# A two-layer decoder on one core: in-place activations, joined products, and other places in the step lists

## The chip, the core and the metric

The kernel runs on one core of a Trainium2 chip, as a single program. The metric is the device time of that program in microseconds. The engines are TensorE (PE; its weight loads are listed apart as PEld), VectorE (DVE), ScalarE (ACT), GpSimd (POOL) and SyncE (SP, which here only issues DMAs). The median of three runs before the change is 2692.59 us (2692.17 to 2693.38).

## The reference

Tokens `x` are 2 batches of 1024, 256 wide, float32. There are two layers of three blocks, each added to a residual stream, each on a LayerNorm of it:

```python
x = x + L0_attn(layernorm(x), ...)             # A: gated delta rule, 4 heads, short convolution of 4 taps
x = x + L0_xattn(layernorm(x), ctx_1024, ...)  # B: cross attention, 16 heads of 64, 154 context tokens
x = x + L0_ffn(layernorm(x), ...)              # C: 8 experts, each takes its own best 512 tokens, GELU, 256-1024-256
x = x + L1_attn(layernorm(x), ...)             # D: rotary attention in a window of 128, 16 heads
x = x + L1_xattn(layernorm(x), ctx_1024, ctx_1024, mask, ...)  # E: masked cross attention, 16 heads of 16
x = x + L1_ffn(layernorm(x), ...)              # F: best 8 of 32 experts per token and 2 shared ones, SiLU, 128 wide
```

In A, `short_conv(hidden @ W)` gives queries, keys and values: a product, then four taps along time, then SiLU. In C, `I` are an expert's best 512 tokens by gate score, and `hid = gelu(ex @ W1 + b1)`.

## The kernel before

The residual stream stays in SBUF as `X`, 16 tiles of 128 tokens. The kernel is six stages, A to F, one after the other. Each has a list `order` of named steps, written out by hand; every engine walks that list in its order and does its share of each step, so an engine that waits in one step delays all its later ones. Semaphores join the engines; a PSUM bank is an object with one semaphore `filled` and one `emptied`.

**LayerNorm** is four steps for a pair of tiles: `stat` (DVE, L257 and L260), then `ln_pool` on POOL (L279, L224 and a Newton step, L213 to L216) for the reciprocal root in `rs`, `norm` (DVE, `xn`, L270), and `ln` (PE, four transposes, L291, then an ACT copy to `XT`, L299). The first LayerNorm waits on POOL for all constants (`const_in`, 48), since the exponent -0.5 is one of them. A LayerNorm for the next stage is spread through the list of the stage before.

**Stage A** (to 810 us) makes 16 channels by 8 blocks of convolution products. One is line 576: for each batch and each half of the 256 inputs a matmul of 128 columns, 4 in all, which the trace records as 8 (each float32 matmul is two records). ACT and DVE then do the taps (L924, L925, L777). Between these run the triangular solves on 64x64 blocks (L664, L674, L678). In the first block four products stand between LayerNorm steps.

**Stage B** (810 to 1170) begins with 8 `value` products (L1232), each beside a LayerNorm, and the first queries (L1241); then scores (L1257) and so on in units.

**Stage C** (1170 to 1488): gate logits, a search of ten digits for each expert's threshold (L1686 on DVE, L1612 on PE), then per expert a `pick` (L1724 makes one-hot tiles, L1629 multiplies them with token numbers), a gather of the tokens by indirect DMA (POOL, L1833), and `turn` (transposes L1636, ACT copy, and a subtraction, L1744, for the low half). Products are taken in three parts with operands split into a high and a low half (`fp32r`); `split` makes the halves of weights on POOL (L1822) or DVE (L1738). An expert's 8 parts, f = 0 to 7, are each `up` (L1569), GELU and `down`, two parts later:

```python
c.e.activation(hid[j % NH_][:, :], b.ap, ACT.Gelu, bias=b1[:, j:j + 1])
c.e.activation(hp[j % NH_][:, 0], b.ap, ACT.Gelu, bias=b1[:, j:j + 1]).then_inc(b.emptied, 1)
```

The first is the whole result in SBUF, the second its high half; DVE (L1752) subtracts the two for the low half.

**Stages D and E** (1488 to 1808 to 2077) are attention in steps of a group g: scores, a maximum on DVE (D: L2040, E: L2373 and L2376), exponentials on ACT, transposes (E: L2315) with DVE copies (E: L2382), products with the values (E: L2326). Each step list also carries `norm` and `ln` for the stage that follows.

**Stage F** (2077 to 2694) runs all 34 experts over all tokens: 136 parts of `up` and `down`, all on line 2559. Weights are split by ACT (L2709) and POOL (L2738), tokens by ACT and DVE. The choice of 8 of 32 is made on DVE in 8 pieces, `route`, one per part from the fourth part on; it is needed from part 8, since the shared experts come first. DVE adds results to `X` (L2694, L2696).

## Time and profile before

| | us |
|---|---|
| median of the runs (n = 3) | 2692.59 |
| profiled execution, its own time | 2696.3 |
| its span | 2694.5 |
| PE busy | 2315.0 (86%) |
| DVE busy | 1662.2 (62%) |
| ACT busy | 1166.5 (43%) |
| POOL busy | 740.6 (27%) |

The granted TensorE clock was 0.929 of full speed on average. The page's row of that clock by 40 slices reads `8699999999999999967999799998997899999999`: it is under full speed in the first slices and around the stage borders. Busy shares are an average over stages with different limits; the chain of waits, which is followed back from the last instruction, tells which engine was last in each stretch. A span is some 2 us shorter than the execution's own time; both are of one execution.

### The profile page before, as it was taken

What the parts mean: (1) busy time and instruction counts of PE and PEld (TensorE: products, weight loads), DVE (VectorE), ACT (ScalarE), POOL (GpSimd) and SP (SyncE); (2) the same over time, 40 slices, a digit from 0 to 9 for tenths busy, and PEclk for the clock granted to TensorE, in tenths of its full rate; (3) what the DMA queues carried; (4) which work ended last, traced back from release to release, by engine and by line L of the source; (5) the groups of instructions that cost most, each with busy time, mean ns of one, the idle gap of its engine ahead of it and who ended that gap; (6) DMA issues with size and microseconds to landing.
All of it is one profiled execution on the core that took longest, in us unless ns stands there. A gap on an engine that the chain in (4) does not pass through costs nothing.

```text
span 2694.5 us, 63114 instructions
## 1 busy us (share of the span) xinstructions
PE 2315.0 (86%) x26243; PEld 1928.3 (72%) x26243; DVE 1662.2 (62%) x3601; ACT 1166.5 (43%) x3232; POOL 740.6 (27%) x875
## 2 busy tenths in 40 slices
PE   4689989998988999946888588888876899999998
PEld 3678878887865777735887366666655688888887
DVE  4566666667644555556774455556665777777776
ACT  2544444444323545412554356556665333333332
POOL 2334243423323333332665433420001011111110
PEclk8699999999999999967999799998997899999999
DMA  2201010101003000021342300000000000000000
GB/s 87 66 10 34 26 34 10 34 26 38 34 2 105 9 17 17 17 71 41 101 106 32 99 2 1 2 2 1 2 1 8 18 18 24 25 26 27 26 7 32
DMA packets 87821, 83.41 MB, mean 31 GB/s; under 512 B 27248, under 2 KB 83312, under 8 KB 86128
## 3 DMA queue, kind: packets, MB, share of 16 engines
q1 hardware_dynamic: 81392, 70.98, 8.5%
q0 software_dynamic: 6144, 8.39, 1.8%
q8 instruction: 208, 3.41, 0.5%
q14 instruction: 77, 0.63, 0.1%
HBM read 68.71 MB, written 10.65 MB: 29 GB/s over the span
## 4 chain that ended last, share of the span: by engine, by line
PE 66%; DVE 17%; POOL 6%; issue 5%; ACT 4%; DMA 1%; DVEq 0%; SPq 0%; ACTq 0%; POOLq 0%
PE bank L2559 20%; PE bank L1569 5%; PE bank L576 4%; PE bank L664 3%; PE bank L678 2%; PE bank L674 2%; PE bank L1291 2%; PE bank L1268 2%; PE bank L1241 2%; DVE d_mx L2040 2%; PE bank L1281 2%; DVE e_P L2373 1%; DVE a_acc L777 1%; PE bank L2315 1%; PE bank L2326 1%
## 5 line engine op out<-in xcount | busy, mean ns | idle before, releaser
L2559 PE MATMUL bank<-f_XH,f_wp 128*128 128x512 f32 x1088 | 366.6, 398 | 8.0 <-POOL f_wp L2738 8.0
L777 DVE SCALAR_TENSOR_TENSOR a_acc<-a_praw,a_convw,a_acc 128x256 f32<-128x256 f32 x345 | 205.0, 595 | 101.3 <-ACT a_acc L925 93.0
L2559 PEld LDWEIGHTS bank<-f_XH,f_wp 128*128 128x128 f32 x1088 | 209.3, 192 | 51.1 <-POOL f_wp L2738 8.6
L2559 PEld LDWEIGHTS bank<-f_wp,f_Hp 128*128 128x128 f32 x1632 | 214.6, 192 | 23.8 <-DVE X L2696 9.6
L2559 PE MATMUL bank<-f_wp,f_Hp 128*128 128x256 f32 x1632 | 219.1, 284 | 12.2 <-DVE X L2696 8.9
L2559 PE MATMUL bank<-f_XL,f_wp 128*128 128x512 f32 x544 | 216.7, 398 | 0.0
L2694 DVE SCALAR_TENSOR_TENSOR X<-bank,f_w,X 128x256 f32<-128x256 f32 x512 | 211.3, 475 | 0.0
L2738 POOL TENSOR_TENSOR f_wp<-wa,f_wp 128x768 fp32r<-128x768 f32 x34 | 62.7, 1845 | 511.4 <-ACT f_wp L2709 511.4
L2732 ACT ACTIVATE f_Hp<-f_H 128x512 fp32r<-128x512 f32 x136 | 85.9, 632 | 222.9 <-DVE f_H L2681 222.9
L576 PE MATMUL bank<-XT,wa 128*128 128x128 f32 x1024 | 165.2, 313 | 7.5 <-ACT a_acc L925 6.6
L2730 ACT ACTIVATE f_G<-bank 128x512 f32<-128x512 f32 x136 | 81.4, 599 | 166.8 <-PE bank L2559 166.8
L576 PEld LDWEIGHTS bank<-XT,wa 128*128 128x128 f32 x1024 | 142.3, 216 | 15.8 <-ACT a_acc L925 7.6
L2683 DVE TENSOR_TENSOR f_Hp<-f_H,f_Hp 128x512 fp32r<-128x512 f32 x136 | 94.1, 692 | 94.9 <-ACT f_Hp L2732 94.9
L664 PE MATMUL bank<-wa 64*64 64x64 f32 x2560 | 108.1, 229 | 44.4 <-DVE wa L866 31.2
L2040 DVE TENSOR_REDUCE d_mx<-bank 128x2 f32<-128x512 f32 (+1 forms) x128 | 75.2, 650 | 115.1 <-PE bank L1976 115.1
L2681 DVE TENSOR_TENSOR f_H<-bank,f_G 128x512 f32<-128x512 f32 x136 | 94.0, 691 | 82.4 <-PE bank L2559 79.0
L291 PE MATMUL bank<-wide,xn 128*128 128x128 f32 x192 | 39.3, 341 | 114.3 <-DVE xn L270 114.3
L664 PEld LDWEIGHTS bank<-wa 64*64 64x64 f32 x2560 | 89.2, 139 | 63.1 <-DVE wa L866 38.1
L2110 ACT ACTIVATE d_P<-bank,d_mx 128x256 f32<-128x256 f32 (+1 forms) x256 | 95.1, 479 | 74.5 <-DVE d_mx L2040 74.5
L992 ACT ACTIVATE wa<-bank 128x256 f32<-128x256 f32 x160 | 58.6, 386 | 157.0 <-PE bank L664 156.2
L279 POOL TENSOR_SCALAR rs<-mv 128x2 f32<-128x2 f32 x48 | 10.9, 226 | 415.9 <-DVE mv L260 403.9
L1390 POOL TENSOR_TENSOR b_P<-b_P,b_rec 128x616 f32<-128x616 f32 x64 | 77.6, 1212 | 172.4 <-DVE b_rec L1328 172.4
(370 smaller groups left out, 5657.2 us busy)
## 6 DMA issues: line engine op xcount, KB each, us to landing
wa<-in_c_w SPq DMA_DIRECT2D x64, 256.0 KB, 3.2
wa<-in_f_gu SPq DMA_DIRECT2D x34, 256.0 KB, 2.8
wb<-grown SPq DMA_DIRECT2D x4, 1536.0 KB, 6.9
a_KQg<-grown SPq DMA_DIRECT2D x4, 1536.0 KB, 6.3
wa<-in_f_d SPq DMA_DIRECT2D x34, 128.0 KB, 2.9
a_E<-decays SPq DMA_DIRECT2D x16, 256.0 KB, 4.8
X<-in_x SPq DMA_DIRECT2D x4, 512.0 KB, 5.7
wa<-in_a_wqkv SPq DMA_DIRECT2D x1, 2048.0 KB, 12.1
```

The costliest lines, as they stand in the source:

```text
L576: i = t.e.matmul(b.ap[:, bb * BT_:(bb + 1) * BT_], wqkv[:, j, c * P:(c + 1) * P], XT[:, j, bb * T + n * BT_:bb * T + (n + 1) * BT_], start ...
L664: i = t.e.matmul(heads(b.ap)[both(bb), h, :], nt[c % 2][both(bb), h, :], xx[c % 2][both(bb), 0, h, :], start=True, stop=True, tile_positio ...
L777: i = v.e.scalar_tensor_tensor(A_, praw[:, c, :, j:j + BT_], convw[:, c, j:j + 1], A_, ALU.mult, ALU.add)
L1569: i = t.e.matmul(out_, lhsT[x], rhs[y], start=first and n == 0, stop=last and n == 2, skip_group_check=True)
L2040: v.e.tensor_reduce(mx[:, of(g, r), :], pair(b.ap)[:, :, lo:], AX, ALU.max, negate=True).then_inc(max_ready.sem, 1)
L2110: i = c.e.activation(Pm[of(g, r)][:, j, lo:], pair(b.ap)[:, j, lo:], ACT.Exp, bias=mx[:, of(g, r), j:j + 1])
L2559: i = t.e.matmul(out_, lhsT[x], rhs[y], start=n == 0 and k == 0, stop=n == 2 and k == nk - 1, skip_group_check=True)
L2681: v.e.tensor_tensor(hid[i][:, :], up.ap, gate[i][:, :], ALU.mult).then_inc(up.emptied, 1)
L2683: v.e.tensor_tensor(hp[i][:, 1], hid[i][:, :], whole(hp[i][:, 0]), ALU.subtract).then_inc(parts_ready.sem, 1)
L2694: i = v.e.scalar_tensor_tensor(X[:, n, :], part, w_[:, n, e_:e_ + 1], X[:, n, :], ALU.mult, ALU.add)
L2730: c.e.activation(gate[i][:, :], b.ap, ACT.Silu).then_inc(b.emptied, 1)
L2732: c.e.activation(hp[i][:, 0], hid[i][:, :], ACT.Copy).then_inc(high_ready.sem, 1)
```

## The change

It has nine edits, by stage. Line numbers in the changed kernel are 5 to 12 higher than before.

- A, start: -0.5 is a tile that POOL sets; the identity has its own DMA; the LayerNorm steps stand together, and the four products after `z` and `gates` 0.
- A: one convolution matmul covers both batches (2 matmuls of 256 columns for 4 of 128). Two late `gate` steps stand one place earlier.
- B: all `stat` steps first, then per pair `value`, `ln`, `norm` and a query.
- C, start: four weight splits ahead of the logits. The pick goes tile by tile with a wait per quarter; token numbers come already multiplied by 128.
- C: GELU's high half first, then GELU in place in the PSUM bank; DVE subtracts from the bank, and the buffer `hid` is gone. `turn` at f = 4 and 5 instead of 5 and 6.
- D, start: the wait for the window mask is at the first score; DVE's cast and POOL's memsets stand behind the first LayerNorms.
- D and E: each `ln` for the stage that follows stands one step later than its `norm`.
- E to F: the last `stat` is in F behind the first split; the last `norm` and `ln` one part later; `route` from part 4, two pieces per part.

```diff
+        minus_half = sb("minus_half", [P, 1])
...
-            for i in (0, 2, 1, 3):
+            def load_x(i):
                 tiles = slice(i * NT // 4, (i + 1) * NT // 4)
                 y.e.dma_start(X[:, tiles, :], a["x"].rearrange("b (t p) d -> p (b t) d", p=P)[:, tiles, :]).then_inc(x_in[i], 16)
-            y.e.dma_start(wide[:, :], a["wide"]).then_inc(const_in, 16)
+
+            load_x(0)
+            y.e.dma_start(wide[:, 0:P], a["wide"][:, 0:P]).then_inc(ident_in, 16)
+            for i in (2, 1, 3):
+                load_x(i)
+            y.e.dma_start(wide[:, P:], a["wide"][:, P:]).then_inc(const_in, 16)
...
-            half = const("half")
+            half = minus_half[:, :]
...
-            g.wait_ge(const_in, 48)
+            g.wait_ge(half_ready, 1)
...
-            t.wait_ge(const_in, 48)
+            t.wait_ge(ident_in, 16)
...
-                order += [(what, "A", halves[i - 2]) for what in ("norm", "ln")] * (i > 1) + conv0[i - 6:i - 5] * (i > 5)
-            order += [("z",), ("gates", 0)] + [("gates", 1)] + conv0[4:7] + [("gates", 2), ("rows",)] + conv0[7:11] + silu0[0:4]
+                order += [(what, "A", halves[i - 2]) for what in ("norm", "ln")] * (i > 1)
+            order += [("z",), ("gates", 0)] + conv0[0:4] + [("gates", 1)] + conv0[4:7] + [("gates", 2), ("rows",)] + conv0[7:11] + silu0[0:4]
...
+                    first -= what == "gate" and t > NC - 3
...
-                        for bb in range(B):
-                            for j in range(KD):
-                                i = t.e.matmul(b.ap[:, bb * BT_:(bb + 1) * BT_], wqkv[:, j, c * P:(c + 1) * P],
-                                               XT[:, j, bb * T + n * BT_:bb * T + (n + 1) * BT_],
-                                               start=j == 0, stop=j == KD - 1, skip_group_check=True)
+                        for j in range(KD):
+                            xt = XT[:, j, :].rearrange("p (b t) -> p b t", b=B)[:, :, n * BT_:(n + 1) * BT_]
+                            i = t.e.matmul(b.ap[:, 0:B * BT_].rearrange("p (b t) -> p b t", b=B), wqkv[:, j, c * P:(c + 1) * P], xt,
+                                           start=j == 0, stop=j == KD - 1, skip_group_check=True)
...
-            lns = [[("stat", "B", i)] * (i < NT // 2) + [("norm", "B", i - 2), ("ln", "B", i - 2)] * (i > 1) for i in range(NT // 2 + 2)]
-            for i in range(NT // 2):
-                order += lns[i] + [("value", i // 4, i // 2 % 2, i % 2)]
-                if i > 2:
-                    order += [("query", 0, m) for m in range(MT) if i > 6 or m == i - 3]
-            order = [s for i, s in enumerate(order) if s not in order[:i]]
-            order += lns[-2] + lns[-1]
+            order += [("stat", "B", i) for i in range(NT // 2)] + [("norm", "B", 0), ("ln", "B", 0), ("norm", "B", 1)]
+            for i in range(MT):
+                order += [("value", i // 4, i // 2 % 2, i % 2)] + [("ln", "B", i + 1)] * (i + 1 < NT // 2)
+                order += [("norm", "B", i + 2)] * (i + 2 < NT // 2) + [("query", 0, i)]
...
-                    if f in (5, 6) and more:
-                        work += [("turn", e_ + 1, 2 * (f - 5))]
+                    if f in (4, 5) and more:
+                        work += [("turn", e_ + 1, 2 * (f - 4))]
...
-            order = [("norm", "C", NT // 2 - 1), ("ln", "C", NT // 2 - 1), ("logits",), ("flip",), ("split", 0), ("split", 1), ("split", 2), ("split", 3)]
+            order = [("norm", "C", NT // 2 - 1), ("ln", "C", NT // 2 - 1), ("split", 0), ("split", 1), ("split", 2), ("split", 3), ("logits",), ("flip",)]
...
+                        for n in range(NT):
+                            t.wait_ge(coded.sem, coded.at[e_, 4 * n // NT])
+                            for m in range(SB):
...
-                        v.step(v.e.scalar_tensor_tensor(idf[:, e_, :], picked[:, :, 0], float(P), idf[:, e_, :], ALU.mult,
-                                                        ALU.add)); v.settle()
-                        v.e.tensor_copy(idx[:, e_, :], idf[:, e_, :]).then_inc(index_ready.sem, 1)
+                        v.e.tensor_tensor(idx[:, e_, :], picked[:, :, 0], idf[:, e_, :], ALU.add).then_inc(index_ready.sem, 1)
...
-                        emptied(v, *s)
-                        v.e.tensor_tensor(hp[j % NH_][:, 1], hid[j % NH_][:, :], whole(hp[j % NH_][:, 0]),
-                                          ALU.subtract).then_inc(parts_ready.sem, 1)
+                        v.wait_ge(hidden.sem, hidden.at[e_, f])
+                        v.e.tensor_tensor(hp[j % NH_][:, 1], b.ap, whole(hp[j % NH_][:, 0]), ALU.subtract).then_inc(b.emptied, 1)
...
-                        c.e.activation(hid[j % NH_][:, :], b.ap, ACT.Gelu, bias=b1[:, j:j + 1])
-                        c.e.activation(hp[j % NH_][:, 0], b.ap, ACT.Gelu, bias=b1[:, j:j + 1]).then_inc(b.emptied, 1)
+                        c.e.activation(hp[j % NH_][:, 0], b.ap, ACT.Gelu, bias=b1[:, j:j + 1])
+                        c.e.activation(b.ap, b.ap, ACT.Gelu, bias=b1[:, j:j + 1]).then_inc(hidden.sem, 1)
...
-                    order += [("norm", "E", (g - 7) // 4), ("ln", "E", (g - 7) // 4)]
+                    order += [("norm", "E", (g - 7) // 4)]
+                if g % 4 == 0 and 0 <= g // 4 - 2 < NT // 2 - 1:
+                    order += [("ln", "E", g // 4 - 2)]
...
+                        t.wait_ge(window_ready, 1)
...
+                    if s == ("keys", 0, 0):
+                        v.e.tensor_copy(smallb[:, :], small[:, 0:3 * P]).then_inc(window_ready, 1)
...
+                    if s == ("project", 0):
+                        for i in range(2):
...
-                    order += [("norm", "F", (g - 7) // 4), ("ln", "F", (g - 7) // 4)]
+                    order += [("norm", "F", (g - 7) // 4)]
+                if g % 4 == 0 and 0 <= g // 4 - 2 < NT // 2 - 1:
+                    order += [("ln", "F", g // 4 - 2)]
...
-            order = [("split", 0)] + [("high", q) for q in range(3)]
+            order = [("split", 0), ("high", 0), ("stat", "F", NT // 2 - 1), ("high", 1), ("high", 2)]
             for p in range(NP + LAG):
-                if p == 1:
+                if p == 2:
                     order += [("norm", "F", NT // 2 - 1), ("ln", "F", NT // 2 - 1)]
-                elif p == 2:
+                elif p == 3:
                     order += [("high", 3), ("logits",)]
-                elif p == 3:
+                elif p == 4:
                     order += [("flip",)]
                 if p < NP:
                     if p % 4 == 2 and p // 4 + 1 < NEX:
                         order += [("split", p // 4 + 1)]
                     order += [("up", p)]
-                    if 3 <= p < 3 + ROUTE:
-                        order += [("route", p - 3)]
+                    if 4 <= p < 4 + ROUTE // 2:
+                        order += [("route", 2 * (p - 4)), ("route", 2 * (p - 4) + 1)]
...
-                for j in range(NEX):
+                for s in order:
+                    if s[0] == "stat":
+                        ln_pool(g, s)
+                    if s[0] != "split":
+                        continue
+                    j = s[1]
```

PE at the start of stage B before. L1232 is `value`, L291 the LayerNorm transposes, L1241 the queries:

```order
L1221 MATMUL bank<-ctxT,wa 128x308 x16
L1232 MATMUL bank<-wa,ctxT 77x512 x4
L291 MATMUL bank<-wide,xn 128x128 x4
L1232 MATMUL bank<-wa,ctxT 77x512 x2
L291 MATMUL bank<-wide,xn 128x128 x4
L1232 MATMUL bank<-wa,ctxT 77x512 x2
L1241 MATMUL bank<-XT,wb 128x256 x2
L291 MATMUL bank<-wide,xn 128x128 x4
L1232 MATMUL bank<-wa,ctxT 77x512 x2
L1241 MATMUL bank<-XT,wb 128x256 x2
```

And the same place after, where the lines are L1237, L296 and L1246:

```order
L1226 MATMUL bank<-ctxT,wa 128x308 x16
L296 MATMUL bank<-wide,xn 128x128 x4
L1237 MATMUL bank<-wa,ctxT 77x512 x2
L296 MATMUL bank<-wide,xn 128x128 x4
L1246 MATMUL bank<-XT,wb 128x256 x2
L1237 MATMUL bank<-wa,ctxT 77x512 x2
L296 MATMUL bank<-wide,xn 128x128 x4
L1246 MATMUL bank<-XT,wb 128x256 x2
L1237 MATMUL bank<-wa,ctxT 77x512 x2
```

The transposes that stood alone between two values now have a query behind them, and the first LayerNorm stands ahead of the values.

DVE in stage C over one expert, before; L1752 is the subtraction for GELU's low half, L1744 the turn:

```order
L1752 TENSOR_TENSOR c_hp<-c_h,c_hp 128x512
L1724 TENSOR_SCALAR c_oh<-c_iota,c_rk 128x512 x4
L1738 TENSOR_TENSOR c_wp<-wa,c_wp 128x1024
L1752 TENSOR_TENSOR c_hp<-c_h,c_hp 128x512
L1724 TENSOR_SCALAR c_oh<-c_iota,c_rk 128x512 x4
L1744 TENSOR_TENSOR c_exT<-bank,c_exT 128x2x256
L1752 TENSOR_TENSOR c_hp<-c_h,c_hp 128x512
L1744 TENSOR_TENSOR c_exT<-bank,c_exT 128x2x256
L1752 TENSOR_TENSOR c_hp<-c_h,c_hp 128x512 x2
```

And after, where they are L1755 and L1747:

```order
L1755 TENSOR_TENSOR c_hp<-bank,c_hp 128x512
L1729 TENSOR_SCALAR c_oh<-c_iota,c_rk 128x512 x4
L1741 TENSOR_TENSOR c_wp<-wa,c_wp 128x1024
L1747 TENSOR_TENSOR c_exT<-bank,c_exT 128x2x256
L1755 TENSOR_TENSOR c_hp<-bank,c_hp 128x512
L1729 TENSOR_SCALAR c_oh<-c_iota,c_rk 128x512 x4
L1747 TENSOR_TENSOR c_exT<-bank,c_exT 128x2x256
L1755 TENSOR_TENSOR c_hp<-bank,c_hp 128x512 x3
```

The subtraction reads `bank` where it read `c_h`, and the turn stands ahead of the subtraction and the one-hot tiles that it followed.

PE in stage E before; L291 is the LayerNorm of stage F, L2315 the turn of the exponentials, L2345 the output product:

```order
L2315 MATMUL bank<-wide,e_P 77x128 x8
L2334 MATMUL bank<-wide,e_OT 128x128 x2
L291 MATMUL bank<-wide,xn 128x128 x4
L2315 MATMUL bank<-wide,e_P 77x128 x8
L2326 MATMUL bank<-e_PT,e_V 32x128 x16
L2304 MATMUL bank<-e_KT,e_Q 128x154 x8
L2340 MATMUL bank<-wide,e_AO 128x128 x2
L2315 MATMUL bank<-wide,e_P 77x128 x8
L2334 MATMUL bank<-wide,e_OT 128x128 x2
L2345 MATMUL bank<-wb_d,e_AOT 128x256 x2
```

And after, L296, L2322 and L2352:

```order
L2322 MATMUL bank<-wide,e_P 77x128 x8
L2341 MATMUL bank<-wide,e_OT 128x128 x2
L2322 MATMUL bank<-wide,e_P 77x128 x8
L2333 MATMUL bank<-e_PT,e_V 32x128 x16
L2311 MATMUL bank<-e_KT,e_Q 128x154 x8
L2347 MATMUL bank<-wide,e_AO 128x128 x2
L2322 MATMUL bank<-wide,e_P 77x128 x8
L2341 MATMUL bank<-wide,e_OT 128x128 x2
L2352 MATMUL bank<-wb_d,e_AOT 128x256 x2
L296 MATMUL bank<-wide,xn 128x128 x4
L2322 MATMUL bank<-wide,e_P 77x128 x8
```

The LayerNorm stands behind the output product of the next step.

## Rows read from the trace of the kernel before

**Rows 1.** The page: the chain of waits by engine.

```profile
PE 66%; DVE 17%; POOL 6%; issue 5%; ACT 4%; DMA 1%; DVEq 0%; SPq 0%; ACTq 0%; POOLq 0%
```

**Rows 2.** By stretch: us, busy us of PE, PEld, DVE, ACT, POOL, PEclk, DMA.

```profile
110.00:810.00 700.00, 630.44 (x12623) 559.78 (x12623) 452.02 (x923) 287.79 (x1075) 241.12 (x273) 0.94 0.08 24
...
1230.00:1488.00 258.00, 213.91 (x1708) 190.92 (x1705) 168.32 (x270) 116.83 (x173) 132.77 (x78) 0.90 0.33 76
```

**Rows 3.** Chain at the start of A: start us, us, what.

```profile
12.31 0.24 POOL rs L279
...
14.53 0.24 POOL rs L279
...
32.20 1.72 PE bank L576 x8
...
45.64 4.14 PE bank L589 x126
...
54.53 0.79 PE bank L599 x2
```

**Rows 4.** Line 257, the LayerNorm statistics, in the first 60 us.

```profile
L257 DVE BATCH_NORM_STATS2 stats<-X x16: 395/410/427, 4.7 to 29.7; 128x6 f32<-128x256 f32 x16
```

**Rows 5.** Chain inside stage A's steady part.

```profile
376.30 1.09 PE bank L576 x8
```

**Rows 6.** Chain inside stage B: products 256 columns wide.

```profile
902.64 1.06 PE bank L1241 x4
...
923.47 3.45 PE bank L1291 x16
```

**Rows 7.** Chain at the start of stage B.

```profile
844.71 0.66 PE bank L291 x4
845.36 1.73 PE bank L1232 x4
...
849.42 0.66 PE bank L291 x4
...
856.12 0.72 PE bank L1257 x8
```

**Rows 8.** Line 1686, the digit count: ns min/median/max.

```profile
L1686 DVE TENSOR_TENSOR c_ges<-c_SN,c_cands x20: 616/624/2830, 1179.1 to 1211.5; 128x448 bf16<-128x448 f32 x20
```

**Rows 9.** Groups on DVE in 1230:1488: busy us, mean ns, idle before.

```profile
L1752 DVE TENSOR_TENSOR c_hp<-c_h,c_hp 128x512 fp32r<-128x512 f32 x64 | 73.4, 1147 | 65.7 <-ACT c_hp L1802 37.9 <-PE bank L1569 27.6
...
L1744 DVE TENSOR_TENSOR c_exT<-bank,c_exT 128x512 fp32r<-128x512 f32 x16 | 10.9, 682 | 6.6 <-ACT c_exT L1791 6.6
```

**Rows 10.** Chain at a change of expert, 1325:1332.

```profile
1329.16 2.90 PE bank L1569 x6
```

**Rows 11.** Waits in 1200:1480: us in total, times, longest.

```profile
PE bank L1569 <- DVE c_exT L1744: 18.9, 6, 3.5
```

**Rows 12.** Chain at the start of stage D.

```profile
1496.25 3.70 PE bank L1953 x4
```

**Rows 13.** Waits of PE in stage D, 1550:1780.

```profile
PE bank L291 <- DVE xn L270: 8.7, 7, 1.2
```

**Rows 14.** Waits of PE in stage E, 1840:2070.

```profile
PE bank L291 <- DVE xn L270: 22.2, 7, 4.4
```

**Rows 15.** Chain in stage E over two steps.

```profile
1989.74 0.49 DVE e_P L2373
...
1996.58 0.49 DVE e_P L2373
...
2006.76 0.49 DVE e_P L2373
```

**Rows 16.** Chain at the start of stage F.

```profile
2078.80 0.23 POOL rs L279
...
2083.25 1.77 POOL f_wp L2738
2085.06 5.42 PE bank L2559 x12
```

More of the change, by code:

```diff
@@ L65, in constant_arrays @@
     c["block"] = (row[:, None] == free[None, :]).astype(f)
-    c["half"] = np.full((P, 1), -0.5, f)
     c["par"] = np.stack([par == 0, par == 1], 1).astype(f)
@@ L432, in stage_a @@
                                                 (6, 2, "ot", 0), (6, 4, "ot", 1)):
+                    first -= what == "gate" and t > NC - 3
                     n = (t - first) // 4
-                    if (t - first) % 4 == 0 and 0 <= n < NB:
+                    if (t - first) % 4 == 0 and 0 <= n < NB and (what, 2 * n + half) not in order:
                         fill[slot] += [(what, 2 * n + half)]
@@ L1181, in stage_b @@
                     out_home["B", s[1]] = banks[i]
+            s = ("value", 1, 1, 1)
+            values_used.append((at[s].filled, at[s].at[("B",) + s]))
             last = at["out", NT - 1]
@@ L1433, in stage_c @@
             NH_, LAG = 3, 2
-            hid = [t_(f"h{i}", [P, CAP]) for i in range(NH_)]
             hp = [t_(f"hp{i}", [P, 2, CAP], F32R) for i in range(NH_)]
@@ L1494, in stage_c @@
                 elif what == "up":
-                    parts_ready.mark(*s[1:])
+                    hidden.mark(*s[1:])
                 elif what == "scatter":
@@ L1546, in sync @@
                 for u in range(NR // 2):
-                    ln_filled(y, "B", NT // 2 - 1)
+                    for values, count in values_used:
+                        y.wait_ge(values, count)
                     fetch(y, u)
@@ L1624, in tensor @@
                         e_ = s[1]
[L1625 removed]
                         t.wait_ge(listed.sem, listed.n)
[L1627 to L1628 removed]
+                        for n in range(NT):
+                            t.wait_ge(coded.sem, coded.at[e_, 4 * n // NT])
+                            for m in range(SB):
                                 i = t.e.matmul(b.ap[:, m * 5:m * 5 + 5], oh[:, n, m * P:(m + 1) * P], info[:, e_, n, :],
[L1630 removed]
+                                               start=n == 0 and m == 0, stop=n == NT - 1, skip_group_check=True)
                     elif what == "turn":
@@ L2212, in stage_e @@
                 if g % 2 == 0:
-                    order += [("out", n)] * (0 <= n < NT) + [("stat", "F", n // 2)] * (0 <= n < NT and n % 2)
+                    order += [("out", n)] * (0 <= n < NT) + [("stat", "F", n // 2)] * (0 <= n < NT - 1 and n % 2)
                 elif g // 8 + 1 < NT // 4:
@@ L2509, in stage_f @@
                 what = s[0]
-                if what in ("norm", "ln"):
+                if what in ("stat", "norm", "ln"):
                     plan_ln(s, banks[7])
@@ L2663, in vector @@
                     what, b = s[0], at.get(s)
-                    if what == "norm":
+                    if what in ("stat", "norm"):
                         ln_dve(v, s)
```

27 lines of the change are left out of this document (10 added, 17 removed).

## The prediction

> **What bounds the kernel now.** I read the chain of waits of the page first: PE holds 66% of it, DVE 17%, POOL 6%, "issue" 5%, ACT 4% [rows 1]. So work taken off PE counts where PE is busy, and elsewhere a shorter wait of PE counts. The table by stretch tells where: in stage A from 110 to 810 PE is busy 630 of 700 us at a clock of 0.94; in stage C from 1230 to 1488 it is busy only 214 of 258, at 0.90, with DVE at 168 and POOL at 133 [rows 2]. Then I read the chain at each border and PE's waits inside stages C, D and E, since nearly all edits are there. All times below are of the profiled execution (2696.3 us, 3.7 above the median of the runs); a difference worked out from it is taken from the median of 2692.6.
>
> **Start of stage A.** The reciprocal roots on POOL start at 12.31 us, one pair every 2.22 [rows 3], yet the statistics start at 4.7 and take 0.41 each [rows 4]. With -0.5 set by POOL itself, the first root can start at about 5.8 (two statistics and their mean, some 1.1). Eight pairs at 2.22 end at 23.5, and the norm, the transposes and the copy at about 26. `z` takes 4.14 (before it began at 45.64 [rows 3]), to 30; four products at 1.72, their cost at the lower clock [rows 3], to 37; the gates' chain took 54.53 less 49.78, so 4.75, after `z` and now shares DVE and ACT with the four products' taps: the first gates' product comes at about 41.5 instead of 54.5. **-13**, between -8 (ACT's copies start only with the late constants) and -16.
>
> **Products of two batches.** There are 128, of which 112 stand in the part where PE is last. One takes 1.09 us for 8 records of 128 columns [rows 5]. The new one is 4 records of 256. I have two rows of that shape: 0.216 us a record in a row of 16 (3.45), so 0.86 for four, but 1.06 where four stand alone among other work [rows 6]. In stage A the product stands alone among small products, as the second row does: 1.06, so -0.03 each, -3.4 in all; with 0.86 it is -0.23 each, -26. I take **-5**, near the first. At the lower clock nothing changes, as 8 records at 1.72 are 0.215 each, twice the 0.107 of 128 columns. The Trainium skill speaks to this (TensorE: Matmul & The Clock Gate, "Back-to-back issue gap"): it gives an isolated gap of N/2.4 + 2.5 ns. An estimate by that page is 8 gaps of 56 ns against 4 of 109, 0.45 and 0.44 us: the columns cost the same however they are cut, and the sum would have 1 us here. The trace has both 0.03 and 0.23 as possible.
>
> **Two late gates.** One of the two leaves the tail of A: **-1** (0 to -4; it shares the tail with others and only one POOL operation is ahead of it).
>
> **Start of stage B.** Before, a pair took 4.71 us from one group of transposes (844.71) to the next (849.42), with `value` at 1.73 and transposes at 0.66 in it, so 2.3 us in which PE waits for DVE's value copy, statistics and norm [rows 7]. Eight queries' 3.45 follow at the end, and scores start at 856.12. With all statistics done ahead, and a query in each step, a step is 1.73 + 0.66 + 0.86 and a little: 3.3. From 820 eight are 26, so scores come at about 846: **-10** (-5 to -11). POOL's roots, 2.2 a pair from about 812, stay ahead of PE's 3.3. Queued behind them is nothing that PE waits for.
>
> **Start of stage C.** The digit count reads two SBUF operands and takes 0.62 us, but up to 2.83 [rows 8], when POOL splits weights beside it; three or four of its 20 are so long, some 7 us in all. Splits ahead of the logits fall to about half on work that the digits don't wait for: **-4** with the wait per quarter of the pick (0 to -9).
>
> **Stage C, experts.** The subtraction L1752 has a mean of 1147 ns over 64, while the same shape with one operand in a bank, L1744, has 682 [rows 9]: 64 x 0.465 is 30 us of DVE time. PE waits 18.9 us in six changes of expert for the turned tokens, 3.5 at most [rows 11], and restarts at the lower clock (6 records in 2.90 us [rows 10], 1.45 more than at full clock). Five such changes cost 5 x (3.5 + 1.45) = 25 us. New: the subtraction reads the bank, DVE has 30 us less, and the turn stands a part (about 3 us) earlier. What is late next is the gather: the turn at f = 4 may stand before it has landed. I charge 5 us for six. **-20**, between -3 (the wait for the gather takes the place) and -27. ACT's second GELU writes a bank; no row shows it. From the rows of ACT (116.8 busy of 258 [rows 2]) it could cost half as much again without being last: 0. The Trainium skill says (SBUF — State Buffer, "SBUF: two separate sides") that a DVE operation with two SBUF inputs and a GpSimd operation take one shared pair of ports, each for its whole length; by that page 0.465 goes wholly for L1752, but the DVE splits of weights and the copies in a fast mode keep stalling. Here 1147 against 682 ns agrees for the first.
>
> **Start of stage D.** DVE's cast and POOL's memsets leave the way of the first LayerNorm, 1.8 us or so; but the first product of D at 1496.25 [rows 12] also waited for the last weight DMA, of which the wait ended just before it: **-1** (0 to -2).
>
> **`ln` a step later, in D and E.** In D PE waits 8.7 us in seven places for DVE's norm [rows 13]; all of it goes and the transposes cost the same: **-8** (-4 to -11). In E it waits 22.2 in seven [rows 14], and the chain goes by DVE's `e_P`: a step without LayerNorm is 6.84 us (1989.74 to 1996.58), one with it 10.18 (1996.58 to 2006.76) [rows 15], so 3.3 more. The norm itself (0.74 on DVE) and the transposes (0.66) remain, but beside other work. 7 x 2.7 = 19 if both are half hidden, 7 x 1 = 7 if the next wait in the step, which is DVE's, is only reached earlier: **-15** (-5 to -22).
>
> **Start of stage F.** POOL runs the last roots from 2078.80 and only then the first split (2083.25, 1.77), so PE starts at 2085.06 [rows 16]. With the split first, PE starts at about 2081: -4, and -2.5 where PE waited for the last norm. `route` moves a part later and is packed into four parts: An estimate from the DVE pieces between 2110 and 2158: 28 us of routing, and 2.8 per part, come to 39 beside PE's 17 instead of 50 beside 33, so PE loses some 5 more. Net **-2** (-8 to +6). The steady rest of F is untouched.
>
> **Sum:** -13 - 5 - 1 - 10 - 4 - 20 - 1 - 8 - 15 - 2 = -79. 2692.6 - 79 = **2614 us**.
>
> **Rivals.**
> (a) The joined product runs at the streaming price, 0.86. For it: the next weight load has 213 ns to hide beneath instead of 107. Against: 1.06 where four stand alone. It gives 21 us more: 2593.
> (b) The stalls in C and E change their name: the gather has not landed at f = 4, and in E DVE's chain is the bound. For it: DVE and not PE leads the chain in E, and in C six gathers are issued only after the index. Against: PE waits 3.5 for `c_exT` by name and not for the gather. C gives -5 for -20, and E -5 for -15: 2639.
> (c) Slower: the joined operand is two runs of 128 tokens that lie 1024 apart. If the engine pays for each run what it paid for a separate product, with a full weight load for each, a product costs 2 x 1.09 = 2.18. That is 1.09 x 112 = 122 more, less 74 for all other edits: +48, 2741. It decides from (74 / 112) + 1.09 = 1.75 us a product. Against: an access pattern of two levels is one instruction, and the number of records in its list of instructions halves. No row shows this very form.
> (d) The start and the borders do not do what they say, since another DMA is last there (constants, weights): A -8, B -5, D 0, F +6, the rest as summed: -79 + 5 + 5 + 1 + 8 = -60, 2633.
>
> **Chances.** Forecast 45%, (a) 16%, (b) 20%, (d) 15%, (c) 3%, and 1% for no change. The range for 8 in 10 is 2585 to 2648. No change that a measurement can tell is within 0.2%, some 5.4 us: only a mix of (c) and the forecast lies there. Faster 0.96, same 0.01, slower 0.03.
>
> **What would show it.** In the changed profile: the first root at about 6 us and the gates' product at 41; the joined product at 1.06 (or 0.86) in the chain; scores of B at about 36 us after its keys began instead of 45; L1752's successor at 0.69 with no maximum of 3 us, and no wait of PE for `c_exT` of 3.5, or in its place one for the gather; steps of 7.5 to 8 us where E has an `ln`; PE in F from 6 us after the last addition of E, not 8. It is wrong if PE's clock in A falls, if ACT's GELU into the bank goes over 1.2 us, or if routing stalls PE by over 15 us.

## The result, and the profile after

The changed kernel takes 2615.81 us (median of 4 runs, 2614.96 to 2623.52), the kernel before 2692.43 (median of 4, 2692.17 to 2693.38). The ratio is 0.9721, with a 95% interval of 0.9703 to 0.974. The profiled span is 2614.3 us against 2694.5, so 80.2 us shorter.

Where they went is read by landmarks: the first or last instruction of a named line in the two traces, and the distance from one to the next. The forecast column has the terms of the sum. "C's first turned tokens" is the start of DVE's first subtraction of the turn (L1744, then L1747), "C's last result" the end of DVE's last write of an expert's output.

| from, to | before | after | difference | forecast |
|---|---|---|---|---|
| start, first gates product of A | 54.53 | 45.33 | -9.2 | -13 |
| to the end of A | 756.02 | 755.38 | -0.6 | -6 |
| to B's first scores | 45.50 | 33.98 | -11.5 | -10 |
| to B's last output product | 309.60 | 313.11 | +3.5 | 0 |
| to C's first turned tokens | 77.84 | 73.47 | -4.4 | -4 |
| to C's last result | 231.90 | 211.15 | -20.7 | -20 |
| to D's first scores | 43.70 | 42.66 | -1.0 | -1 |
| to E's first scores | 303.98 | 292.30 | -11.7 | -8 |
| to E's last output product | 253.98 | 227.69 | -26.3 | -15 |
| to the end of F | 617.44 | 619.23 | +1.8 | -2 |

The chain of waits of the changed kernel goes back only to about 2000 us, where the trace lacks a link, so earlier stretches are read from timelines and waits. First POOL and PE at the start (start us, length, engine, what, and in brackets the idle time before and what ended it), which answers to [rows 3]:

```profile
5.89 0.23 POOL L284 TENSOR_SCALAR rs<-mv 128x2 f32<-128x2 f32 x1 [4.49 <-DVE mv L265]
...
25.22 1.11 PE L296 MATMUL bank<-wide,xn 128*128 128x128 f32 x4 [1.09 <-DVE xn L275]
...
27.11 7.01 PE L594 MATMUL bank<-wa,XT 128*64 128x12 f32 x128 [0.78 <-ACT XT L304]
...
34.05 6.29 PE L582 MATMUL bank<-XT,wa 128*128 128x256 f32 x16
```

And, in the same timeline, the first gates product:

```profile
45.33 0.79 PE L604 MATMUL bank<-a_E,wide 128*128 128x128 f32 x2 [4.99 <-DVE a_E L804]
```

The roots start at 5.89, as estimated, and the transposes end at 26.3. Then `z` takes 7.01 us where it took 4.14 before: it is now the first long piece of PE's work, and its 128 records take 55 ns each where they took 32, so it ran at the lower of the clock's two levels (1.2 and 2.4 GHz) here and at the higher before. The profile's clock column reads 1.00 in this stretch, as it does ahead of the first change that it records; but that first change is a rise, at 39.3 us, behind `z`. Before, four products had run ahead of `z`, and the first recorded rise is at 45.7 us, where `z` begins.

Stage C: the subtraction for GELU's low half (now L1755) and the digit count (now L1691), ns min/median/max, answering to [rows 8, 9]:

```profile
L1755 DVE TENSOR_TENSOR c_hp<-bank,c_hp x64: 671/691/695, 1228.5 to 1427.6; 128x512 fp32r<-128x512 f32 x64
```

The digit count:

```profile
L1691 DVE TENSOR_TENSOR c_ges<-c_SN,c_cands x20: 618/624/891, 1165.5 to 1190.7; 128x448 bf16<-128x448 f32 x20
```

Neither has a long tail here; the maximum of the subtraction was 3451 ns. (In five later profiles with the same start of C one count of the 20 takes 2.66 to 2.71 us; the digits are 0.2 us longer there.) PE's waits from the first turned tokens to the last result, answering to [rows 11]:

```profile
PE bank L1641 <- DMA c_ex<-normed,c_idx: 4.2, 7, 1.7
PE bank L1574 <- DVE c_exT L1747: 1.5, 1, 1.5
```

The 18.9 us of waiting for turned tokens are 1.5, and 4.2 us of waiting for the gather are new. The prediction named both, and charged 5 us for the second, which is where the experiments found more.

Stage E by stretch: first before, then after, from first to last scores (columns as in [rows 2]):

```profile
1823.10:2059.50 236.40, 191.11 (x2176) 146.12 (x2176) 156.67 (x391) 157.69 (x402) 17.83 (x44) 0.88 0.01 1
```

After:

```profile
1767.40:1980.40 213.00, 173.99 (x2176) 131.59 (x2176) 156.82 (x391) 155.58 (x402) 17.87 (x44) 0.97 0.01 2
```

The instructions are the same 2176, but PE is busy 174 us and not 191, and the granted clock is 0.97 instead of 0.88. Of PE's waits in the same two stretches, before:

```profile
PE bank L291 <- DVE xn L270: 17.8, 6, 4.4
PE bank L2315 <- DVE e_PT L2382: 12.4, 16, 1.4
```

After:

```profile
PE bank L2322 <- DVE e_PT L2389: 20.1, 24, 1.1
```

The wait for the norm is gone, but waits under other names grew by 11.6 us, so that all waits together fell by 6.2 only (45.3 to 39.1). The other 17.1 us of this stretch are PE's busy time, which is shorter at the higher clock. How much of both is the edit's own is left to the experiments.

PE's waits in F's first 90 us, before and after:

```profile
PE bank L2559 <- DVE X L2696: 8.9, 3, 3.6
PE bank L2559 <- POOL f_wp L2738: 8.0, 1, 8.0
...
PE bank L2559 <- DVE X L2694: 2.5, 1, 2.5
```

After:

```profile
PE bank L2566 <- DVE X L2703: 16.3, 3, 9.8
PE bank L2566 <- issue: 4.5, 1, 4.5
```

The start wait went from 8.0 to 4.5, and the waits for DVE during the routing from 11.4 in four to 16.3 in three, one of 9.8 (and 1.4 for the tokens' low half, L2676).

### The profile page after: what moved, and what is told of

It reads as the page before. It is cut to its first block and busy times, and to the rows that moved or that the text cites. A ratio compares the mean times of both kernels' runs of the same rounds, so it can differ in the third digit from the quotient of the medians.

```text
span 2614.3 us, 62054 instructions
## 1 busy us (share of the span) xinstructions
PE 2287.6 (88%) x25731; PEld 1873.6 (72%) x25731; DVE 1641.1 (63%) x3593; ACT 1163.2 (44%) x3232; POOL 735.1 (28%) x876
## 5 line engine op out<-in xcount | busy, mean ns | idle before, releaser
L2566 PE MATMUL bank<-f_wp,f_Hp 128*128 128x256 f32 x1632 | 219.3, 284 | 17.2 <-DVE X L2703 16.3
L582 PE MATMUL bank<-XT,wa 128*128 128x256 f32 x512 | 160.5, 446 | 7.6 <-ACT a_acc L930 6.6
L2044 DVE TENSOR_REDUCE d_mx<-bank 128x2 f32<-128x512 f32 (+1 forms) x128 | 75.2, 650 | 106.6 <-PE bank L1979 106.6
L582 PEld LDWEIGHTS bank<-XT,wa 128*128 128x128 f32 x512 | 100.0, 215 | 28.3 <-ACT a_acc L930 8.9
L2566 PEld LDWEIGHTS bank<-f_XL,f_wp 128*128 128x128 f32 x544 | 104.8, 193 | 16.9
L2432 ACT ACTIVATE e_P<-e_P,e_mx 128x154 f32<-128x154 f32 x256 | 90.7, 415 | 50.2 <-DVE e_mx L2383 50.2
```

Of the source, the lines that this page charges most:

```text
L582: i = t.e.matmul(b.ap[:, 0:B * BT_].rearrange("p (b t) -> p b t", b=B), wqkv[:, j, c * P:(c + 1) * P], xt, start=j == 0, stop=j == KD - 1, ...
L2432: i = c.e.activation(p_[:, j, :], p_[:, j, :], ACT.Exp, bias=mx[:, of(g, r), j:j + 1])
L2566: i = t.e.matmul(out_, lhsT[x], rhs[y], start=n == 0 and k == 0, stop=n == 2 and k == nk - 1, skip_group_check=True)
```

## The experiments

Each whole time is a median, and each ratio is to the kernel before, run beside it on the same chip. Single executions differ by some 5 us even where the code is equal: stage A from its first gates product to the first product with its state took 94.7 us in the profile of the changed kernel, at a clock of 0.71, and 89.2 in that of another (GELU back in SBUF) whose code is the same there. So each experiment is read in the stage that it touches, and its whole time beside that.

**Two products again.**

```diff
-                        for j in range(KD):
-                            xt = XT[:, j, :].rearrange(...)[:, :, n * BT_:(n + 1) * BT_]
-                            i = t.e.matmul(b.ap[:, 0:B * BT_]..., wqkv[:, j, c * P:(c + 1) * P], xt, ...)
+                        for bb in range(B):
+                            for j in range(KD):
+                                i = t.e.matmul(b.ap[:, bb * BT_:(bb + 1) * BT_], wqkv[:, j, c * P:(c + 1) * P],
+                                               XT[:, j, bb * T + n * BT_:bb * T + (n + 1) * BT_], ...)
```

> The changed kernel with the convolution product of stage A as before: four matmuls of 128 columns, eight records, instead of two of 256. Theory 1 (a product that stands alone costs 1.06 us joined and 1.09 apart): stage A from its first to its last product longer by 112 x 0.03 = 3 us at most, time 2616 to 2619. Rival (the joined product runs at the streaming price of 0.86 and the gain was eaten elsewhere): longer by up to 26 us, 2640.

Measured: 2617.23 us (2610.84 to 2621.37), ratio 0.9734 (0.9717 to 0.9751). From the first product with the state to the end of the convolutions 545.6 us, against 541.6 joined; but four other runs with the joined product have 544.0 to 546.0 there. PE on this line alone, 520 us of stage A, apart and then joined (us, busy us and records of PE and of the weight loads, clock):

```profile
160.00:680.00 520.00, 116.67 (x755) 98.00 (x753) 0.94 0.09 27
```

And joined:

```profile
160.00:680.00 520.00, 114.71 (x380) 68.73 (x380) 0.94 0.09 27
```

That is 116.67 / 755 x 8 = 1.24 us a product apart, and 114.71 / 380 x 4 = 1.21 joined. The rival of 0.86 is refuted, and so is the slower rival of 1.75 and more: two runs of columns far apart cost PE nothing. The joined product is worth 0.03 us each, which this measurement of the whole cannot tell from nothing. PE's weight loads are busy 69 us instead of 98, and the busy time of the products shows nothing of it.

**Stage C: where GELU is written, and when the turn stands.** Three kernels: GELU back to SBUF; the turn back at 5 and 6; and both. The first edit moves only the result and DVE's operand: DVE's subtraction still releases the bank, and the high half still comes first, as in the changed kernel.

```diff
-                        c.e.activation(b.ap, b.ap, ACT.Gelu, bias=b1[:, j:j + 1]).then_inc(hidden.sem, 1)
+                        c.e.activation(hid[j % NH_][:, :], b.ap, ACT.Gelu, bias=b1[:, j:j + 1]).then_inc(hidden.sem, 1)
```

```diff
-                    if f in (4, 5) and more:
-                        work += [("turn", e_ + 1, 2 * (f - 4))]
+                    if f in (5, 6) and more:
+                        work += [("turn", e_ + 1, 2 * (f - 5))]
```

> The changed kernel, but ACT's second GELU writes a buffer in SBUF again, and DVE subtracts two SBUF operands; the turn stays at f = 4 and 5. Theory 1 (the stall of DVE beside POOL is most of the gain in stage C): the subtraction has a mean over 1.0 us again, PE waits for the turned tokens or the hidden parts, 10 to 20 us more, 2626 to 2636. Rival (the earlier turn is most of it): the subtraction stalls, but PE doesn't wait, 0 to 5 us more.

> The changed kernel with the turn at f = 5 and 6, as before; GELU stays in its bank. Theory 1 (the freed DVE time is most of the gain): PE waits for the turned tokens 0 to 1 us an expert, 0 to 5 us more, and the small waits for the gather at f = 4 (4.3 us over seven) go: between -4 and +5. Rival (the place of the turn is most of it): 3 us of wait and a restart at the lower clock in each of five changes of expert, 15 to 20 us more.

> The changed kernel with both undone in stage C: the second GELU in SBUF and the turn at f = 5 and 6. Both theories: the 21 us that stage C gained between the first turned tokens and the last result are lost, 2637. What is told apart is the sum: if the other two runs lose together about as much as this one, the edits add; if this one loses much more than their sum, either alone suffices.

Measured, from the first turned tokens to C's last result, and in whole:

| GELU | turn | stretch us | whole us (range) | ratio (interval) |
|---|---|---|---|---|
| bank | 4, 5 (the change) | 211.2 | 2615.81 (2614.96 to 2623.52) | 0.9721 (0.9703 to 0.974) |
| SBUF | 4, 5 | 217.3 | 2617.96 (2614.29 to 2621.7) | 0.9736 (0.972 to 0.9753) |
| bank | 5, 6 | 204.9 | 2611.38 (2606.3 to 2612.78) | 0.9703 (0.9685 to 0.9721) |
| SBUF | 5, 6 | 228.6 | 2633.85 (2627.96 to 2642.12) | 0.9783 (0.9765 to 0.9801) |

The two edits do not add. With GELU in SBUF, the earlier turn saves 11.3 us; with GELU in the bank it costs 6.3. The bank alone is worth 23.7 us, more than both together (17.4). So with the turn late, theory 1 holds, and a little more than it said (6.3 us shorter, 4 at most expected); with the turn early, both stories for `hid_sbuf` fall short: the subtraction stalls, and the stretch is 6.1 us longer, where theory 1 had 10 to 20 and the rival 0 to 5.

With both undone, what PE waits for at the changes of expert is back. The view gives it no name:

```profile
PE bank L1575 <- issue: 16.6, 5, 3.4
```

One of the five in its timelines, on DVE, POOL and PE:

```profile
1306.51 3.45 DVE L1756 TENSOR_TENSOR c_hp<-c_h,c_hp 128x512 fp32r<-128x512 f32 x1
...
1306.47 2.93 POOL L1824 TENSOR_TENSOR c_wp<-wa,c_wp 128x1024 fp32r<-128x1024 f32 x1
...
1310.66 2.82 PE L1575 MATMUL bank<-c_exT,c_wp 128*128 128x512 f32 x6 [3.31 <-issue]
```

The subtraction lies beside a weight split of POOL and takes 3.45 us instead of 0.69, and it stands between the two halves of the turn (at 1305.91 and 1309.88), which PE needs. That holds in all: of the 64 subtractions 11 take 3.0 to 3.45 us, here and in the kernel before, each beside a split of POOL, and the 27 that no POOL instruction overlaps take 0.695 us at most. With the bank, 42 of 64 overlap POOL, and none takes more than 0.695. In the kernel before, five of the long ones stand in that place, at the five waits of 3.5 us for the turned tokens.

DVE's subtraction, with SBUF and a late turn:

```profile
L1756 DVE TENSOR_TENSOR c_hp<-c_h,c_hp 128x512 fp32r<-128x512 f32 x64 | 73.4, 1147 | 62.6 <-ACT c_h L1804 32.0 <-PE bank L1575 26.2 <-issue 4.3
```

And with the bank and a late turn:

```profile
L1755 DVE TENSOR_TENSOR c_hp<-bank,c_hp 128x512 fp32r<-128x512 f32 x64 | 44.0, 688 | 58.4 <-PE bank L1574 35.9 <-ACT bank L1803 18.4 <-issue 4.1
```

ACT's second GELU, in the first and in the second of these:

```profile
L1804 ACT ACTIVATE c_h<-bank,c_b 128x512 f32<-128x512 f32 x64 | 43.6, 681 | 0.0
```

The second:

```profile
L1803 ACT ACTIVATE bank<-bank,c_b 128x512 f32<-128x512 f32 x64 | 41.7, 652 | 0.0
```

With the bank DVE is 29 us less busy on this line, and 20 in the whole stretch (160.8 to 140.8): 9 of them come back on the one-hot tiles (L1729, mean 596 ns against 502), five of which now meet the splits and take 2.1 to 2.2 us, where PE does not wait for them. ACT's in-place GELU is no dearer (652 ns against 681). In the late run with the bank no wait for the gather is listed, and 1.5 us for turned tokens is all; in the early one the gather costs 4.2 us, and PE is busy 1.5 us longer (203.8 against 202.3). Those two make 5.7 of the 6.3 us.

**Stage E: the LayerNorm in the step of its norm, and the same with filled waits.**

```diff
-                    order += [("norm", "F", (g - 7) // 4)]
-                if g % 4 == 0 and 0 <= g // 4 - 2 < NT // 2 - 1:
-                    order += [("ln", "F", g // 4 - 2)]
+                    order += [("norm", "F", (g - 7) // 4), ("ln", "F", (g - 7) // 4)]
```

The second kernel adds, in `ln_pe` ahead of the wait for `xn_ready`:

```diff
+            if k == "F" and n2 < NT // 2 - 1:
+                t.wait_ge(b.emptied, b.at["ln", k, n2] - 1)
+                for _ in range(12):
+                    t.e.matmul(b.ap[:, 0:P], ident, ident, start=True, stop=True, skip_group_check=True)
```

> The changed kernel with stage E's LayerNorm transposes in the same step as their norm again (stage D's stay a step later). Theory 1 (the wait for the norm and the lower clock after it): stage E from its first to its last scores goes from 213 to about 236 us, its granted clock from 0.97 back to 0.88, and the time is 22 to 26 us more. Rival (only the wait counts, and the rest of E's gain came from the query or the output products that moved against it): 10 to 15 us more, with the clock at 0.97.

> As ln_same, but PE fills the wait for the norm: 12 additional products of the identity (128 columns, 24 records, about 2.6 us at full clock), written to the LayerNorm's bank ahead of the transposes, which overwrite it. The output is unchanged, and 7 x 12 products are added. Theory 1 (half of the loss is the lower clock): clock 0.95 or more, and the time is below ln_same by 6 to 12 us although PE has more to do. Rival (the wait alone): as ln_same or up to 5 us more.

Measured: 2635.76 us (2632.78 to 2641.53; ratio 0.9798, 0.9782 to 0.9814) and 2628.89 (2622.15 to 2634.08; 0.9765, 0.9744 to 0.9787). From E's first to its last scores: 229.0 and 223.5 us, against 213.0 changed and 236.4 before. Theory 1 for the first had 236 at a clock of 0.88, and its rival 10 to 15 us more at 0.97: it came out between, 16.0 more at 0.95. Theory 1 for the second (6 to 12 us below the first, by the whole times 6.9) holds. PE's row of the two (the first, then the filled one):

```profile
1766.50:1995.50 229.00, 178.76 (x2176) 135.27 (x2175) 156.86 (x391) 157.35 (x402) 17.87 (x44) 0.95 0.01 2
```

And the filled one:

```profile
1768.10:1991.70 223.60, 189.88 (x2320) 148.10 (x2320) 156.87 (x391) 156.47 (x402) 18.53 (x44) 0.97 0.01 2
```

The filled run has 144 records more and is busy 11 us longer, and yet ends 5.5 us sooner. The distance between the maxima of neighbouring groups tells why, step by step:

| kernel | step without LayerNorm | step with the wait | step with the late transposes |
|---|---|---|---|
| before | 6.8 | 8.9 once, 10.2 to 11.6 in five | |
| LayerNorm in the norm's step | 6.8 | 8.9 in two, 10.5 in four | |
| the same, filled | 6.8 | 8.9 in all six | |
| changed | 6.8 | | 7.3 in six |

So one LayerNorm costs 0.5 us late; in the same step it costs 2.1, and 3.7 where PE's clock falls. In two steps at 1.6 and four at 3.2 more than late, that is the 16.0 us. PE's wait for the norm is 2.7 us in five of the six and 4.4 in one, and a fall of the clock begins within 0.7 us of its end in four. Filling kept the clock.

**Both attention stages undone.** The same edit in stage D too.

> The changed kernel with the LayerNorm transposes in the same step as their norm in both attention stages, D and E. Theory 1 (the wait, and in some of them the lower clock): D from its first to its last scores goes from 264.4 to 272 to 273 us (273.1 before, and 273.0 with D untouched), E to 229 as in the run that undid E alone: 24 us more than the changed kernel in these two. Rival for the 7 us of E that neither wait nor step explains (the late transposes of D are what brings PE into E at full clock): E goes to 236 here.

Measured: 2650.03 us (2646.56 to 2654.9; 0.9858, 0.9842 to 0.9875). D from first to last scores 273.7 us against 264.4 changed (263.0 to 266.1 in the runs that have its late transposes); from there to E's first scores 32.7 against 27.9; E 229.2. So D's edit is worth 9.3 us in its steps, and 3.0 to 4.8 at the border (30.9 us before). E does not go to 236: that rival is refuted. E before was 7 us longer still; 4.4 of these are in its first eight steps (59.4 us against 55.0), where the clock of before was 0.85, against 0.94 in the run that undid E alone. There is one profile of the kernel before, and whether it would meet that again stays open.

**Routing spread again.**

```diff
-                    if 4 <= p < 4 + ROUTE // 2:
-                        order += [("route", 2 * (p - 4)), ("route", 2 * (p - 4) + 1)]
+                    if 3 <= p < 3 + ROUTE:
+                        order += [("route", p - 3)]
```

with the last `norm` and `ln`, logits and flip one part earlier, as before.

> The changed kernel with stage F's routing as before (one piece per part from part 3 to 10, the last LayerNorm at part 1, the logits at part 2); the first weight split still stands ahead of the last statistics. Theory 1 (packing two pieces into a part makes one wait of 9.8 us out of several of 2 to 3.6): F is 4 to 6 us shorter, 2610 to 2612. Rival (the longer stretch comes from the later start and not from the packing, and DVE's sum is the bound in either): within 2 us of the changed kernel.

Measured: 2612.1 us (2608.53 to 2618.76; 0.9706, 0.9688 to 0.9725). F's first 12 parts take 75.5 us instead of 81.2 (75.2 before; eight other runs with packed routing have 79.0 to 80.3, one 81.2). PE's waits there are those of before, 9.0 in three and 2.5 once. The four profiles with spread routing have 75.2 to 76.5, so the packing cost 2.5 to 6 us.

**z behind the four products.**

```diff
-            order += [("z",), ("gates", 0)] + conv0[0:4] + [("gates", 1)] + ...
+            order += conv0[0:4] + [("z",), ("gates", 0), ("gates", 1)] + ...
```

> The changed kernel with the first four convolution products of stage A ahead of the gate product z and of gates 0, instead of behind them. Theory 1 (whatever is first after the LayerNorms runs at half clock, and z took 7.0 us there against 4.1 before): z falls to about 4.1, while the four products keep their 6.3, and the gates' product comes about as early or 1 to 2 us earlier, since its chain of 4.7 us now lies bare: between -3 and +2. Rival (the clock does not matter, the chain of the gates does): 4 us more.

Measured: 2610.46 us (2607.8 to 2613.9; 0.9701, 0.9685 to 0.9717). The first gates product stands at 40.81 instead of 45.33:

```profile
26.23 5.97 PE L582 MATMUL bank<-XT,wa 128*128 128x256 f32 x16
32.13 3.91 PE L594 MATMUL bank<-wa,XT 128*64 128x12 f32 x128
40.81 0.80 PE L604 MATMUL bank<-a_E,wide 128*128 128x128 f32 x2 [4.77 <-DVE a_E L804]
```

`z` takes 3.91 us behind the products and 7.01 ahead of them; the products 5.97 and 6.29. The first rise of the clock that this profile records is at 31.0 us, ahead of `z`, where it was at 39.3, behind it. The 4.5 us by which the gates are sooner, more than theory 1 had, are these: `z` is 3.1 us shorter, PE's work begins 0.9 sooner (26.23 against 27.11), the products are 0.3 shorter, and the last wait 0.2.

That last wait is equal in the two for different reasons. Here the chain of the gates lies bare behind `z` and takes 4.8 us. In the changed kernel it takes 11.2 us from the end of `z`, beside the products, because DVE does their taps in the middle of it (the second line is DVE's next link of the gates' chain):

```profile
37.92 5.84 DVE L782 SCALAR_TENSOR_TENSOR a_kn<-a_praw,a_convw,a_kn 128x256 f32<-128x256 f32 x12 [2.82 <-ACT a_kn L930]
43.67 0.22 DVE L801 TENSOR_SCALAR a_E<-a_E 128x128 f32<-128x128 f32 x1
```

**Two parts alone on the kernel before.** GELU in the bank (with its waits), and E's LayerNorm a step later; both diffs stand above.

> The kernel before with two parts of the change alone: GELU in place in its bank, and stage E's LayerNorm transposes a step later. Theory 1: stage C from the first turned tokens to the last result goes from 231.9 us to 205, and stage E from its first to its last scores from 236.4 to 213, the rest as before: 2642 to 2646. Rival for E (7 of its 23 us were the phase in which the kernel before met the falls of the clock, and not the edit): E goes to 213 all the same, but stages A, B and D of this run, whose code is that of before, differ from the profile of before by several us either way. Rival for C (the bank needs the turn at f = 4): C stays above 215.

Measured: 2650.57 us (2645.12 to 2654.61; 0.9837, 0.9819 to 0.9855). C's stretch 206.0 us against 231.9, E's 213.6 against 236.4: 43 us in the span from two edits of a few lines. The rival for C is refuted. The whole is 5 us above the 2642 to 2646 of theory 1: stage A, whose code is that of before, is 4.8 us longer, so single executions do differ by several us, as the rival for E said; E itself goes to the same 213 to 214 in all runs that have its late transposes.

**Three starts as before.** B's values interleaved with the statistics, C's splits behind the logits, F's first split behind the last statistics.

> The changed kernel with three starts as before: stage B's values interleaved with its statistics, stage C's splits behind the logits, and stage F's first split behind the last statistics. Theory 1, by stage: B from the end of A to its first scores 34.0 to 45.5 us (11.5 more); C from its logits to the first one-hot tiles 47.2 to 50.2 (3 more); F's first product 4.5 to 8.0 after E's last (3.5 more): 18 in all, 2634. Rival for C (the splits only change places with the counts, since the overlap with POOL remains): C within 1 us.

Measured: 2630.69 us (2627.49 to 2635.69; 0.9771, 0.9755 to 0.9788). From the end of A to B's first scores 44.7 us against 34.0; from B's first to last scores 293.2 against 295.9; from C's logits to the first one-hot tiles 50.4 against 47.2; F's first product 8.0 after E's last against 4.5. So 10.7, 3.2 and 3.5 us are lost at these starts themselves, near the expectation, and the rival for C is refuted. B's later part is another matter. Against the kernel before, the changed one's last scores stand 3.5 us later behind its first. 0.8 of that comes in the first 32 of the 512 products and is there with the old start too (0.7 in this run), so it is not the start's. The rest, 2.7, comes in the last 21, where the clock falls; in between all profiles keep step within 0.2 us. That last part is 0.1 to 4.7 us in the eleven profiles with the new start, nine of which have the fall, and nothing in the three with the old one, which have none. Whether the new start takes part in it, by where in time it puts B's end, stays open. From the end of A to B's last output product it is worth 5.4 to 10.5 us, and 7.9 in the changed kernel's profile.

**All three better places together**: z behind the products, the turn at 5 and 6, the routing spread.

> The changed kernel with the three edits that were each shorter in their own stage in the last runs: z behind the first four products (4.5 us), the turn at f = 5 and 6 with GELU in the bank (6.3 us), the routing spread over eight parts (4 to 5.7 us). Theory 1 (the stages don't touch each other): 15 us less than the changed kernel, 2600 to 2602. Rival (what one stage gains, the clock at the next border takes): 2604 to 2612.

Measured: 2603.65 us (median of 5, 2601.76 to 2606.42; before 2693.72), ratio 0.9668 (0.9655 to 0.9681). That is clear of the changed kernel's interval, 0.9703 to 0.974, and by the medians 12 us faster. In its profile: 5.3 us at A's gates, 5.2 in C, 4.7 in F's first 12 parts; the rest of stage A then lost 2.4 and the end of E 2.6, where the clock fell at other places. So it is between the two theories.

## Why the prediction was right, step by step

The forecast was 2614 us, measured 2615.8. Most mechanisms were right, and that the sum came so near is luck, since errors of both signs cancelled: A had 9 us too much, F 4 and B 2, while C had 1 and D and E together 15 too little. Of those 15, some 10 are not the edits' work at all: 7.4 us of E's scores in the one profile of the kernel before, which stay open, and 2.9 behind its last scores, a stretch that takes 13.1 to 17.3 us in the runs with late transposes (14.7 in the changed kernel, 17.6 before).

- **Start of A.** The chain of roots went as worked out (5.89 against 5.8, the last transposes at 26.3 against 26). The term that was too short is `z` at 4.14 us: that row stood behind four products, at the clock's upper level, and the new place is behind LayerNorms that left it at the lower. It took 7.01 us; that is 2.9 of the 3.8 us by which the gates' product missed 41.5, and the run with `z` last got 3.1 back.
- **Products of two batches.** The difference was right, 0.03 us each, though busy time gives 1.24 and 1.21 a product and not 1.09 and 1.06. Rival (a)'s 0.23 set a joined product in a stream (0.86) against a separate one that stands alone (1.09). In the trace of [rows 5] the eight records start 0.111 us apart, so eight in a stream would take 0.89 by an estimate from that, and the difference is 0.03 there too.
- **Stage B.** 11.5 us at the first scores, 10 forecast. 0.8 was given back within 14 us (with the old start too, see the three starts), and 2.7 near B's end. There the same wait for POOL, 1.5 us before and 1.58 after, ended at full clock before:

```profile
1141.81 1.10 PE L1268 MATMUL bank<-wide,b_P 128*77 128x128 f32 x8 [1.52 <-POOL b_P L1390]
```

  And at half clock after:

```profile
1116.86 1.10 PE L1273 MATMUL bank<-wide,b_P 128*77 128x128 f32 x8
...
1121.29 1.99 PE L1273 MATMUL bank<-wide,b_P 128*77 128x128 f32 x8 [1.58 <-POOL b_P L1395]
```

- **C's start.** 4.4 against 4. The count's longest is 0.89 us instead of 2.83 (rows above), while the part from the logits to the first count is 4.3 longer: the splits cost there and save 7.3 in the digits.
- **C's experts.** 20.7 against 20, but of its two parts only one was a gain: the bank is worth all of it and more, and the turn's move, which the sum counted as help, costs 6 us where the bank is used. The prediction charged 5 us for the gather, and did not ask whether the turn's move was still needed. It was not.
- **D and E.** E's term of 15 us is near the edit's own share, 16.0 by undoing it alone. But the sum had it as 2.1 for each of seven and named no clock, and the runs show 1.6 in two steps and 3.2 in the four where the clock falls. The waits did change their names in part, as rival (b) said (11.6 us of 17.8). In D it was 9.3 for 8, and the border of D to E gained 3 more.
- **Start of F.** 3.5 of 4 came. The loss by packing was 2.5 to 6 us, 5 forecast, and the wait for the last norm stayed (2.8 us), which had been booked as 2.5 of gain.
- **Rivals.** (a) and (c) are refuted by the run with two products. (d) is refuted for B and F by the starts undone; at the start of A it had 8 us, nearer to the 9.2 measured than the forecast's 13, but by `z` and not by a DMA. Of (b), the gather's wait came and was small, and in E the waits for DVE's copies took a good part of the norm's place.

## What to carry to other kernels

Where a wait of PE is only 2.7 us, ask what its clock does behind it: here the lower clock nearly doubled the price of a LayerNorm's wait (2.1 to 3.7 us), and moving the waiting step behind other work took away both. Where two edits aim at one stall, measure each alone: the second may cost what the first has already paid. And an execution of the same code differs by up to 6 us in a stage, by where the clock falls, so compare stages and not whole times when an edit is worth a few us.

## What the runs showed of the hardware

- ACT's GELU in place in a PSUM bank costs no more than to SBUF: 652 ns against 681, 128x512.
- DVE's subtraction with one operand in a bank stays at 691 ns beside POOL's splits; with both in SBUF its mean is 1.12 to 1.15 us, since 11 of 64 lie beside a split and take 3.0 to 3.45. With the bank the one-hot tiles meet the splits instead, and five take 2.1 us where 0.48 is the median.
- 144 additional records in PE's waits made a stage 5.5 us shorter (223.5 against 229.0), at a clock of 0.97 instead of 0.95.
- `z` of 128 small records: 7.01 us or 3.91, by what PE had done ahead of it.
